# Chunked linear attention beside a mixture of eight experts: state outputs on 64x64 quarters of TensorE, and both row halves of every attention stage in one slot

## What is computed

```python
def step(state, inp):                       # chunks of 64 rows, 8 heads of 32 features
    qq, kk, vv = inp
    inter = einsum('bhcd,bhde->bhce', qq, state)
    scores = einsum('bhcd,bhed->bhce', qq, kk) * mask
    intra = einsum('bhce,bhed->bhcd', scores, vv)
    state = state + einsum('bhcd,bhce->bhde', kk, vv)
    return (state, inter + intra)
z = cumsum(k, axis=1)
denom = maximum(abs(sum(q * z, axis=-1)), 1.0)[..., None]
attention = rmsnorm(o / denom, norm_w) @ Wo

def experts(x):                             # 8 experts, 256 -> 256 -> 256
    weights = routing_weights(x, Wr, temperature)
    h = silu(x @ Wg[e]) * (x @ Wu[e])
    return sum over e of weights[e] * (h @ Wd[e])

x = x + layernorm(attention(layernorm(x)))
x = x + layernorm(experts(layernorm(x)))
```

## Time and profile before

| what | value |
|---|---|
| median of 3 runs | 1539.62 us (1537.99 to 1541.61) |
| the profiled execution | 1541.07 us, span 1539.4 us |
| TensorE busy, instructions | 1504.1 us (98%), 13920 |
| VectorE busy | 1004.3 us (65%) |
| ScalarE busy | 683.2 us (44%) |
| GpSimd busy | 434.3 us (28%) |
| mean granted TensorE clock | 0.994 |

### The profile page before, as it was taken

The page is one execution under the profiler, slowest core; times in us unless marked ns, Lnnn a source line. Parts: engine busy times, 40 slices in busy tenths (PEclk is TensorE's granted clock), DMA queues, the critical chain, the costliest instruction groups (busy, mean ns, idle before and its releaser), DMA issues. The chain is left out here.

```text
span 1539.4 us, 36292 instructions
## 1 busy us (share of the span) xinstructions
PE 1504.1 (98%) x13920; PEld 1288.0 (84%) x13920; DVE 1004.3 (65%) x2388; ACT 683.2 (44%) x1261; POOL 434.3 (28%) x704
## 2 busy tenths in 40 slices
PE   7799999999999999999999999999999999999997
PEld 6688888888888888888888888888888888888886
DVE  5656657666676766757666676666757666666665
ACT  4543444445344453444445344453534445344433
POOL 1422413224141232413224141232413224141231
PEclk9999999999999999999999999999999999999999
DMA  3300000000000000000000000000000000000000
GB/s 117 104 1 2 28 0 14 14 14 14 0 14 14 14 14 0 27 0 14 14 14 14 0 14 14 14 14 0 27 0 14 14 14 14 0 14 16 2 8 21
DMA packets 25344, 24.58 MB, mean 16 GB/s; under 512 B 2016, under 2 KB 25056, under 8 KB 25312
## 3 DMA queue, kind: packets, MB, share of 16 engines
q1 hardware_dynamic: 25312, 24.13, 5.0%
HBM read 15.74 MB, written 8.39 MB: 16 GB/s over the span
## 5 line engine op out<-in xcount | busy, mean ns | idle before, releaser
L923 DVE TENSOR_TENSOR late<-late,up_ps 128x512 f32<-128x512 f32 x256 | 175.0, 684 | 174.1 <-PE up_ps L414 143.9
L414 PE MATMUL down_ps<-w_hi,h_hi 128*128 128x256 f32 x976 | 265.3, 294 | 0.0
L1125 POOL TENSOR_TENSOR rms_f<-rms_in,minus_half 128x16 f32<-128x16 f32 x32 | 93.7, 2929 | 587.2 <-DVE rms_in L887 587.2
L726 ACT ACTIVATE late<-gate_ps 128x512 f32<-128x512 f32 x256 | 152.0, 594 | 239.9 <-PE gate_ps L414 233.9
L414 PE MATMUL down_ps<-w_hi,h_lo 128*128 128x256 f32 x976 | 252.6, 281 | 0.0
L646 ACT ACTIVATE h_hi<-late 128x512 fp32r<-128x512 f32 x256 | 160.7, 628 | 187.4 <-DVE late L923 187.4
L945 DVE SCALAR_TENSOR_TENSOR late<-down_ps,route,late 128x256 f32<-128x256 f32 x364 | 158.8, 478 | 104.6 <-PE down_ps L414 102.1
L839 DVE TENSOR_TENSOR h_lo<-late,h_hi 128x512 fp32r<-128x512 f32 x256 | 175.3, 685 | 66.7 <-ACT h_hi L646 66.7
L414 PE MATMUL gate_ps<-ft_hi,w_hi 128*128 128x512 f32 x512 | 206.3, 403 | 0.6 <-ACT ft_hi L646 0.4
L414 PE MATMUL gate_ps<-ft_hi,w_lo 128*128 128x512 f32 x512 | 203.1, 397 | 0.8 <-issue 0.8
L414 PE MATMUL up_ps<-ft_hi,w_hi 128*128 128x512 f32 x512 | 202.9, 396 | 0.0
(11 more groups left out here) (157 smaller groups left out, 2591.3 us busy)
## 6 DMA issues: line engine op xcount, KB each, us to landing
xs<-in_x SPq DMA_DIRECT2D x32, 256.0 KB, 2.9
out_rows<-late SPq DMA_DIRECT2D x32, 256.0 KB, 2.2
late<-in_wg SPq DMA_DIRECT2D x8, 256.0 KB, 2.9
late<-in_wu SPq DMA_DIRECT2D x8, 256.0 KB, 2.8
late<-in_wd SPq DMA_DIRECT2D x8, 256.0 KB, 2.8
late<-in_wkv_t SPq DMA_DIRECT2D x1, 512.0 KB, 5.1
late<-in_wq_t SPq DMA_DIRECT2D x1, 256.0 KB, 4.2
late<-in_wo_t SPq DMA_DIRECT2D x1, 256.0 KB, 5.8
```

The costliest lines, as they stand in the source:

```text
L414: last = nc.tensor.matmul(dst, lhs, rhs, start=n == 0, stop=n == len(terms + low_terms) - 1)
L726: nc.scalar.activation(h_f[:, m, :], gate_ps[:, :], ACT.Silu).then_inc(silu_ready[0], 1)
L923: nc.vector.tensor_tensor(h_f[:, m, :], h_f[:, m, :], up_ps[m][:, :], ALU.mult).then_inc(h_ready[0], 1)
L1125: nc.gpsimd.tensor_tensor(rms_f[:, p, :, :], rms_in[:, :, :], minus_half[:, :, :], ALU.pow)\
```

## The change

Three things are altered.

1. The state product of `o` runs on 64x64 quarters: 16 matmuls of 66 columns for 8 of 132. The state loses its zero halves and gets five places in place of four; GpSimd copies the fifth to the first once a block (`carry`), and VectorE's state additions wait for that. A product whose two row quarters would write to the same bank is made in two parts: `o_own` (and the scores by the values), then `o_other`, which waits until `o_own` is done. In the blocks of `STEPS` both own parts come first, then both other parts.
2. `STEPS` takes both row halves of `kt`, `su`, `s`, `o`, `ot`, `wo` and `ft` in one slot each. The steps between them move accordingly. Buffers are doubled for that (`kz`, `prob` with its second half in `shared`, `ot_hi`/`ot_lo`, `rms_in`), and small ones share memory to make room (`rz` in `nearer`, `inh` in `tanh`, `expo` and `cube` in `off`).
3. The first block keeps its order of steps, with `carry` added, the split of `o`, and one small matmul (`warm`) between its parts.

The core of the diff:

```diff
@@ STEPS
-    [("kt", 0), ("su", 0)],
+    [("kt", 0), ("kt", 1)],
     [],
-    [("s", 0), ("kt", 1)],
+    [("su", 0), ("su", 1)],
     [],
-    [("o", 0), ("su", 1)],
+    [("s", 0), ("s", 1)],
     [],
-    [("norm_stats", 0), ("s", 1)],
+    [("o", 0), ("norm_stats", 0), ("o", 1)],
+    [],
+    [("norm_stats", 1)],
     [("norm_apply", 0)],
-    [("o", 1), ("ot", 0)],
-    [("norm_stats", 1)],
-    [("wo", 0)],
-    [("norm_apply", 1), ("ln2_stats", 0)],
-    [("ot", 1)],
+    [],
+    [("norm_apply", 1), ("carry",)],
+    [("ot", 0), ("ot", 1)],
+    [],
+    [("wo", 0), ("wo", 1)],
+    [("ln2_stats", 0), ("ln2_stats", 1)],
     [("ln2_apply", 0)],
-    [("wo", 1), ("ln2_add", 0), ("ln3_stats", 0)],
-    [("ln2_stats", 1)],
-    [("ln3_apply", 0), ("ln2_apply", 1)],
-    [("ln2_add", 1), ("ln3_stats", 1)],
-    [("ft", 0)],
+    [("ln2_add", 0), ("ln3_stats", 0), ("ln2_apply", 1), ("ln2_add", 1), ("ln3_stats", 1)],
+    [("ln3_apply", 0)],
     [("ln3_apply", 1)],
-    [("ft", 1), ("ft_out", 0), ("ft_out", 1)],
+    [("ft", 0), ("ft", 1), ("ft_out", 0), ("ft_out", 1)],
     [],
@@ buffers
-        state = sb("state", [P, B, 4, 2, HG * PAIR])
+        state = sb("state", [P, B, 5, HG, PAIR])
@@ tensor
+            def with_state(p, dst, b, x, i):
+                half, tok, c = slice(64 * x, 64 * x + 64), (2 * p + b) * P + C * i, b * HPG * VA + x * PAIR
+                for g in range(HG):
+                    last = nc.tensor.matmul(dst[C * g:C * g + C, i, c:c + PAIR], q_t[half, g, tok:tok + C],
+                                            state[half, b, 2 * p + i, g, :], start=b == 0 and x == i, stop=b == B - 1 and x != i)
+                return last
+            def o_own(p, dst, a):
+                for b in range(B):
+                    for x in range(2):
+                        with_state(p, dst, b, x, x)
...
+            def o_other(p, dst, a):
+                reach(pe, o_own_done, a, p + 1)
+                pe.sem_inc(quarters_begun, 1)
+                for b in range(B):
+                    for x in range(2):
+                        last = with_state(p, dst, b, x, 1 - x)
+                return last
...
+                    o_own(p, dst, a).then_inc(o_own_done[0], 1)
+                    if psum_order(a) is FIRST_PSUM_STEPS:
+                        warm(1)
+                        last = o_other(p, dst, a)
+                    elif p == 0:
+                        return
+                    else:
+                        o_other(0, att_half(("o", 0), a), a).then_inc(att_done[0], 1)
+                        last = o_other(1, dst, a)
@@ vector, su
+                    reach(dve, state_carried, a, 0)
+                    reach(dve, state_ready, a, step[1])
@@ gpsimd
+                elif kind == "carry":
+                    reach(pool, att_done, a, number_of(("o", 0), a) + 1)
+                    reach(pool, state_ready, a, 2)
+                    carried, to = (state[:, :, m, :, :].rearrange("p b g v -> p b (g v)") for m in (4, 0))
+                    nc.gpsimd.tensor_tensor(to, carried, v_sb[:, 0, 0:1, D:VA].broadcast_to([P, B, HG * PAIR]), ALU.mult)\
+                        .then_inc(state_carried[0], 1)
```

More of the change, by code:

```diff
@@ L98 @@
     [("wo", 0)],
-    [("norm_apply", 1), ("ln2_stats", 0)],
+    [("norm_apply", 1), ("carry",), ("ln2_stats", 0)],
     [("ot", 1)],
@@ L316, in att_half, with prob_of @@
             return att_ps[:, 2 * n, :] if step[0] == "q" else att_ps[:, 2 * n:2 * n + 2, 0:columns]
+        def prob_of(p, a):
+            return probs[0 if psum_order(a) is FIRST_PSUM_STEPS else p]
         def is_last(f):
@@ L415, in products, with warm @@
                 return last
+            def with_state(p, dst, b, x, i):
[9 more added lines that the diff above has]
+                for b in range(B):
+                    for j in range(HPG):
+                        for g in range(HG):
+                            for i in range(2):
+                                chunk, c = slice(C * i, C * i + C), b * HPG * VA + j * VA
+                                last = nc.tensor.matmul(dst[C * g:C * g + C, i, c:c + VA],
+                                                        prob_of(p, a)[chunk, j // 2, b, 2 * g + j % 2, :],
+                                                        v_sb[chunk, 2 * p + b, g * HPG + j, :], start=False, stop=False)
+                return last
+            def o_other(p, dst, a):
+                reach(pe, o_own_done, a, p + 1)
+                pe.sem_inc(quarters_begun, 1)
+                for b in range(B):
+                    for x in range(2):
+                        last = with_state(p, dst, b, x, 1 - x)
+                return last
+            def warm(count):
+                for _ in range(count):
+                    nc.tensor.matmul(gate_ps[:, 0:P], ident[:, :], ident[:, :], start=True, stop=True)
             def att_step(step, a):
@@ L468, in att_step @@
                                     last = nc.tensor.matmul(dst[C * i:C * i + C, r, (4 * b + n) * C:(4 * b + n) * C + C],
-                                                            kz[half, g, j, c:c + C], q_t[half, g, tok:tok + C],
+                                                            kz[half, p, g, j, c:c + C], q_t[half, g, tok:tok + C],
                                                             start=True, stop=True)
@@ L598, in rest @@
                 down(E - 1, 1, f)
-            def warm(count):
-                for _ in range(count):
-                    nc.tensor.matmul(gate_ps[:, 0:P], ident[:, :], ident[:, :], start=True, stop=True)
             pe.wait_ge(const_ready, 1)
@@ L678, in att_step @@
                     for j in range(2):
-                        last = nc.scalar.activation(kz[:, :, j, :], src, ACT.Copy, scale=odd_even[:, j:j + 1])
+                        last = nc.scalar.activation(kz[:, step[1], :, j, :], src, ACT.Copy, scale=odd_even[:, j:j + 1])
                     last.then_inc(kz_ready[0], 1)
@@ L691, in att_step @@
                 elif kind == "ot":
-                    copy(ot_hi, src).then_inc(ot_hi_ready[0], 1)
+                    copy(ot_hi[step[1]], src).then_inc(ot_hi_ready[0], 1)
                 elif kind == "wo":
```

55 lines of the change are left out of this document (21 added, 34 removed).

## The result

The changed kernel takes 1530.22 us, the kernel before 1541.2 beside it: ratio 0.9933, 95% interval 0.9919 to 0.9946. The forecast was 1540, no change; the time is inside the stated 1528 to 1552, but the interval leaves no change out. The profiled execution of the changed kernel took 1530.17 us. One more of its six runs, at a mean granted clock of 0.75, took 1807.7 us and is not compared. In the later rounds the kernel before took 1539.7 to 1540.7 us, so the gain is about 10 to 11 us.

The account below looks back on a forecast made before the run. TensorE, busy 98%, was taken as the bound, with an equally long layer-norm chain from `wo` to `ft`. 15 x (2.0 - 1.97) = +0.5 us on 1541.07 gave 1541.6, as a median 1540.0; range 1528 to 1552.

Parts of the forecast that it names:

- TensorE's part: TensorE's attention stages: from 11.40 to 9.43 us a block, a gain of 1.97 us, 29.5 us over 15 blocks.
- The chain from `wo` to `ft`: Layer norms between `wo` and `ft`: second `ft` can run at 17.93 us, a wait of 2.0 us a block.
- The chain with the hold: Between `wo` and `ft`, VectorE's residual sum holds GpSimd's root until 13.55 us; without such a lock, 3 us less in sum.
- What costs nothing: `carry`, the 16 state additions in one slot and the two squares of `o` on ScalarE: no cost.
- The sum: All steady blocks: 15 x (2.0 - 1.97) = +0.5 us, TensorE's gain given back at `ft`.
- the block's period stays at 92.4: Steady blocks: expected sign that one block still takes 92.4 us.
- the gain survives in part: Rival at `ft`: roots free and no VectorE wait for `high`, wait 1.0 us a block, 1525 us; chance 0.31.
- The pairs: Rival at `o`: state matmuls go in pairs, stay at 1.06 us, lose 1.1 a block, 1556 us; chance 0.04.
- The clock: Rival: granted clock falls behind each wait at `ft`, costing 21 us, 1561 us; chance 0.06.
- The price in the prediction (1.4): Some 1.4 us lost at half clock speed behind one wait of 2.43 us, taken 15 times.

Follow-up runs that it names:

- after_placed: The changed kernel with the placement of before_placed; 1524.8 us, ratio 0.9895 to the kernel before.
- before_placed: The kernel before, instructions unchanged, with `ft` and `h` directly behind the experts' weights, at distances 0 and 64 modulo 256; 1523.8 us.
- before_moved: before_placed with 64 unused bytes ahead of `w_hi`, so weights, `ft`, `h` and everything behind lie 64 bytes further; 1522.2 us.
- before_moved_weights: before_placed with the weights 64 bytes further and `ft` and `h` where they were modulo 256; 1542.7 us.
- tail_two_earlier_placed: The changed kernel with most steps between `o` and `ft` moved earlier, layer norms by two slots, `o` and `ft` unmoved, and before_placed's placement; 1535.4 us.
- all_at_64: The changed kernel with 32 unused bytes ahead of `xs` and 32 ahead of `o_sb0`, so every tensor TensorE reads starts at a multiple of 64; 1523.3 us.

## Why the prediction was right and wrong

**TensorE's part** was right: 11.40 us a block was to become 9.43. By the same starts, with the ways in and out, `kt` 0.88, `su` 1.28, `s` 2.24, `o` 3.31, `ot` 0.88 and `ft` 0.87 make 9.46. The agreement in busy time, as said above, was luck.

**The chain from `wo` to `ft`** was right within 0.1 us, in its end, its wait (the stage of `ft` takes 2.79 us in place of 0.87, so 1.9 for 2.0) and its two pieces (the first `ft` starts 0.73 late, for some 0.7). GpSimd's first operation of the root beside VectorE's residual sum in the changed kernel:

```profile
613.76 0.55 POOL L1134 TENSOR_TENSOR shift<-mv,minus_one 128x2 f32<-128x2 f32 x1 [2.63 <-DVE mv L879]
```

```profile
613.60 0.66 DVE L941 TENSOR_TENSOR x<-rows,xs 128x512 f32<-128x512 f32 x1
```

It begins 12.95 us after `wo` (12.96 forecast), takes 0.55 instead of 0.20 and ends 0.05 after VectorE's. The chain with the hold was the right one.

**What costs nothing** held: no wait stands at `s`, `ot` or a down product. But the prediction followed the new long group of VectorE only as far as `ft` and never asked when the `h_lo` behind that group would be there. It was late, and only the new wait at `ft` hid it.

**The sum failed.** It was 15 x (2.0 - 1.97), everything else taken as it was: "gate and up are 1.41 each, a down product 1.42". That the change moved no instruction of the experts was read as: their durations stay. The step that failed is "the block's period stays at 92.4": by their pitches gate, up and down went from 1.40, 1.40 and 1.42 us to 1.39, 1.36 and 1.43, 0.63 us a block, and the period was 91.80. after_placed against before_placed shows the rest of the sum right in total (+0.08 for +0.03), but not to that precision in its terms. With faster experts the old kernel already waits longer at `ft` (0.35 us idle in place of 0.15), so that the change had more to take away there, and some 0.2 us a block more lies outside the attention stages, for which no run here shows a cause. before_placed, before_moved and before_moved_weights show one instruction stream at 1522 to 1543 us by addresses alone.

**The rivals.** The time lies where "the gain survives in part" had it, but that rival's mechanism, a shorter wait at `ft`, did not occur. The pairs fell with the first state matmuls. The clock did not fall in the steady blocks of the changed kernel, where the wait comes in pieces of 0.57 and 0.97 us (every period is 91.80, but for the first, 91.91). It did not even fall where the earlier trace rows had it fall: behind the same wait of 2.43 us ahead of block 1 the granted clock was 1.00:

```profile
79.00:82.00 3.00, 2.78 (x17) 2.46 (x18) 1.71 (x3) 2.25 (x6) 2.39 (x7) 1.00 0.00 0
```

So one fall behind one wait was not a rule. Behind one piece of 2.0 us it fell 6 times out of 15 in tail_two_earlier_placed, at 1.6 us each. The price in the prediction (1.4) was about right, the case for it was another kernel's.

## What to carry to other kernels

When a change resizes or moves buffers, compare the pitch of matmuls that it does not touch before crediting or blaming the edit, and compare both kernels at one placement; here placement alone moved one instruction stream between 1522 and 1543 us, and at one placement the change made 1 us. Try the distance of the moving and the stationary operand in steps of 32 bytes, by a gap of that size. And before freeing a wait, look at when the next instruction's inputs are there: a wait named in the trace may hide another that is nearly as long. And look at the clock behind a wait: behind single waits of 2 us it fell in some blocks here, at 1.6 us each.

## What was not expected of the hardware

- **A matmul's pitch depends on where its two operands lie relative to each other.** 512 columns took 226.7 to 226.9 ns at distance 0 (228.6 with `h` moved), 229.4 at 64 and 231.8 to 233.3 at 32, 96, 128 and 192. 256 columns (down, where the weights move and `h` is stationary) took 119.3 to 119.4 at 0, 118.1 to 118.9 at 32, 96 and 128, and 115.5 to 116.5 at 64. Gate changed less (230.3 to 233.7). The rule is not complete: at one distance of `ft`, up took 226.7 and 228.6 ns with `h` at 0 and at 32. A longer period is not excluded: modulo 512 the distance of `ft` is 256 in the changed kernel and at 0 in before_placed (up 226.7 and 226.8), but that of `h` is 320 in all_at_64 and 64 in before_placed (down 115.5 and 116.2). Only steps of 32 were tried, and which of a matmul's reads meet stays open. The Trainium skill (SBUF — State Buffer, Who interferes with whom) gives TensorE one read port for the moving operand and one for weight loads and calls them independent. The measurement differs from that here, as far as speed goes: one instruction stream changed up's pitch by 3% with the distance of the two operands. The same section of the Trainium skill says that TensorE never waits for anyone; that is about other engines, and no run here tests it.
- **A wait in one piece of 2.0 us** was followed by half speed (granted clock 0.54 over 3 us) in some blocks and not in others of one run, 6 times out of 15, and one of 2.43 us was in the kernel before (0.54) and not in the changed one (1.00).
- **Four quarter matmuls of 66 columns** take 0.13 to 0.14 us for four (0.283 and 0.263 for eight), whichever operand is stationary: `q_t` here, `k_sb` in `su`.
